# Up products of the experts as three products of split 16-bit halves, in a fused attention and mixture-of-experts kernel

## What is computed

```
logits = xf @ router_w
gate_vals, idx = top_k(logits, 2)
gates = softmax(gate_vals)
for e in range(8):
    h = relu(xf @ w1[e] + b1[e]) @ w2[e] + b2[e]
    y = layernorm(xf + h, gamma[e], beta[e])
    out = out + sum(where(idx == e, gates, 0)) * y
```

## Time and profile before

| | us |
|---|---|
| median of 3 runs | 539.31 |
| the profiled execution, its own time | 539.75 |
| its span, from the first to the last instruction | 538.0 |
| TensorE busy | 482.5 |
| VectorE busy | 440.2 |
| ScalarE busy | 366.8 |
| GpSimd busy | 307.6 |

### The profile page before, as it was taken

One profiled execution on the slowest core, in us unless ns is written; L12 is line 12 of the kernel. 1 busy time (PEld: TensorE's weight loads), 2 busy tenths in 40 slices (PEclk: granted clock), 3 DMA queues, 4 the chain that ended last, 5 costly groups with the idle time before them and its releaser, 6 DMA issues.

```text
span 538.0 us, 15851 instructions
## 1 busy us (share of the span) xinstructions
PE 482.5 (90%) x4764; PEld 389.4 (72%) x4764; DVE 440.2 (82%) x1768; ACT 366.8 (68%) x849; POOL 307.6 (57%) x447
## 2 busy tenths in 40 slices
PE   3989999999999999989999899999999999999700
PEld 2866666767666666666666699999899999999700
DVE  5876877997777697978778669989998888879897
ACT  5566567776756767667577566876686787778562
POOL 2542021557784386576876768777776555545420
PEclk9999999999899999999899999999999999999955
DMA  5247744426154322333311674877897788886499
GB/s 148 76 153 234 232 108 136 125 81 190 34 174 125 115 88 93 108 110 116 124 37 33 175 262 132 220 201 208 245 275 234 210 244 244 248 225 213 151 337 260
DMA packets 73590, 90.43 MB, mean 168 GB/s; under 512 B 9262, under 2 KB 57297, under 8 KB 73506
## 3 DMA queue, kind: packets, MB, share of 16 engines
q1 hardware_dynamic: 52626, 66.43, 43.0%
q0 software_dynamic: 6416, 12.93, 6.8%
q10 hardware_dynamic: 14464, 10.06, 6.2%
HBM read 63.25 MB, written 30.79 MB: 175 GB/s over the span
## 4 chain that ended last, share of the span: by engine, by line
PE 36%; issue 21%; POOL 20%; DVE 14%; ACT 3%; DMA 2%; SPq 1%; ACTq 1%; POOLq 0%; DVEq 0%
PE sbk L985 12%; POOL sorted_d L1685 11%; PE avb L997 6%; PE mbk L997 6%; POOL kept L1662 2%; POOL rs L1671 2%; PE mbk L975 1%; PE mbk L860 1%; PE avb L800 1%; DVE stk L1575 1%; PE sbk L827 1%; DMA xins<-in_xp 1%; PE gen L808 1%; DVE pexs L1457 1%; DVE pexs L1487 1%
## 5 line engine op out<-in xcount | busy, mean ns | idle before, releaser
L1685 POOL DMA_INDIRECT sorted_d<-pay,slot x96 | 96.8, 1008 | 35.8 <-issue 25.1
L1188 DVE TENSOR_REDUCE mx<-mbk 128x4 f32<-128x768 f32 x96 | 91.1, 949 | 30.3 <-PE mbk L860 29.9
L1699 POOL DMA_INDIRECT expert_d<-pexs,dest x70 | 70.3, 1004 | 42.6 <-DVE pexs L1487 24.8
L648 ACT ACTIVATE pexs<-sbk 128x768 f32<-128x768 f32 x96 | 77.5, 808 | 22.7 <-PE sbk L887 21.2
L985 PE MATMUL sbk<-pexs 128*128 128x256 f32 (+1 forms) x224 | 50.6, 369 | 0.3 <-ACT pexs L697 0.3
L985 PE MATMUL sbk<-pexs,stk 128*128 128x256 f32 (+1 forms) x224 | 48.3, 358 | 1.2 <-issue 1.1
L697 ACT ACTIVATE pexs<-sbk,xins 128x256 f32<-128x256 f32 (+1 forms) x112 | 43.9, 463 | 7.8 <-PE sbk L985 5.7
L697 ACT ACTIVATE pexs<-sbk,w12s 128x256 f32<-128x256 f32 (+1 forms) x112 | 42.6, 450 | 8.2 <-PE sbk L985 6.9
L1699 POOL DMA_INDIRECT expert_d<-xT,dest x33 | 32.9, 996 | 21.4 <-issue 10.7
L985 PEld LDWEIGHTS sbk<-pexs 128*128 128x128 f32 x224 | 39.0, 190 | 4.4 <-issue 0.5
L1648 POOL TENSOR_TENSOR kept<-hs,lnb 128x384 f32<-128x384 f32 x16 | 16.0, 1000 | 45.2 <-DVE hs L1163 45.1
(11 more groups left out here) (259 smaller groups left out, 1239.5 us busy)
## 6 DMA issues: line engine op xcount, KB each, us to landing
stk<-pack_d SPq DMA_DIRECT2D x28, 512.0 KB
pexs<-pack_d SPq DMA_DIRECT2D x28, 512.0 KB
stack_d<-kqs ACTq DMA_DIRECT2D x48, 192.0 KB, 2.6
stk<-stack_d SPq DMA_DIRECT2D x64, 144.0 KB
xn<-sorted_d SPq DMA_DIRECT2D x47, 132.0 KB
pack_d<-in_w SPq DMA_DIRECT2D x16, 256.0 KB
xins<-in_xp SPq DMA_DIRECT2D x16, 128.0 KB, 3.9
hs<-in_txt SPq DMA_DIRECT2D x16, 128.0 KB, 3.2
```

The lines of the kernel that those rows point to most:

```text
L648: act.activation(pex[p % 2][m][:, :, :], sbk[:, :, 0:COLS], ACT.Exp, scale=0.25).then_inc(a_pex, 1)
L1188: dve.tensor_reduce(dst, mbk[:, :, 0:COLS].rearrange("p h (c s) -> p h c s", c=2), AX.X, ALU.max).then_inc(d_mx, 1)
L1685: pool.indirect_dma_start(sorted_d[:, :], bass.IndirectOffsetOnAxis(ap=slot[p % 6][:, 2 * k + w:2 * k + w + 1], axis=0), pay[p % 6][:, k, ...
L1699: pool.indirect_dma_start(expert_d[:, :], bass.IndirectOffsetOnAxis(ap=dest[fin % DESTS][:, k:k + 1], axis=0), ye[fin % RESULTS][:, k, :], ...
```

## The change

- `w1` is split. For each expert, SyncE loads `w1[e]` into SBUF (`fetch`), ScalarE scales it by 32 and rounds it to 16 bits (`w1_high`), VectorE computes the rest as another 16-bit half (`w1_low`), and `pack` writes both halves to `pack_d`. The halves together have the size of the 32-bit weights. The eight `w1_high` and `w1_low` are put into the lists of the attention stage, and the next `fetch` stands at the end of `pack`.
- The turned rows are split too: ScalarE writes the high half `xh` (where it wrote `xsT`), and VectorE subtracts it from the turned rows in PSUM and writes the low half `xl` (`low`).
- Each up product becomes three products of 16-bit halves: low weights by high rows, high by high, high by low. Relu divides by 32.
- `first` and `dest` go from VectorE to GpSimd, as three operations (`mark`). ScalarE's `norm_row(g)` now also waits for `mark(g - 4)`, since that reads the expert's number from the same buffer.
- The weights go through 6 buffers in place of 8.

The core of the diff:

```diff
-WEIGHTS, NORMS = 8, 4
+WEIGHTS, NORMS = 6, 4
+RAISE = 32.0
...
+            def fetch(e):
+                if e:
+                    sp.wait_ge(w1_split, 2 * e)
+                sp.dma_start(w1_f32, a["w1"][e]).then_inc(w1_in, 16)
+
             def pack(e):
-                sp.dma_start(pack_d[e, :, 0:F], a["w1"][e]).then_inc(pack_out, 16)
+                sp.wait_ge(w1_split, 2 * e + 2)
+                sp.dma_start(pack_d[e, :, 0:F], plans[:, F:2 * F]).then_inc(pack_out, 16)
                 sp.dma_start(pack_d[e, :, F:F + FC * D].rearrange("p (c d) -> p c d", c=FC),
                              a["w2"][e].rearrange("(c p) d -> p c d", p=P)).then_inc(pack_out, 16)
+                if e + 1 < NE:
+                    fetch(e + 1)
...
+            def w1_high(e):
+                act.wait_ge(w1_in, 16 * (e + 1))
+                if e:
+                    act.wait_ge(pack_out, 32 * e)
+                act.activation(w1_f16[:, 0:F], w1_f32, ACT.Copy, scale=RAISE).then_inc(w1_split, 1)
...
                 after(act, b_y, g - NORMS)
+                after(act, b_dest, g - NORMS, 3)
...
-                    act.activation(xsT[nxt % 2][:, 0:n], (bank[6] if nxt else gen_of("b0", 0))[:, 0:n], ACT.Copy).then_inc(b_xs, 1)
+                    act.activation(xh[nxt % 2][:, 0:n], turned_of(nxt)[:, 0:n], ACT.Copy).then_inc(b_xh, 1)
...
-            xt(3); hi(3); vcopy(2); vcopy(3); lo(3); xt(4); xnorm(5); hi(4); mxt(0); xt(5); gexp(6); lo(4); gexp(7)
+            xt(3); hi(3); vcopy(2); vcopy(3); lo(3); xt(4); xnorm(5); hi(4); w1_high(0); mxt(0); xt(5); gexp(6); lo(4); gexp(7)
...
-            context(1, 1); vcopy(5); soft(2, 1); mxt(3); ct(0); soft(2, 2); soft(2, 3); xnorm(9); context(2, 0)
+            context(1, 1); vcopy(5); soft(2, 1); mxt(3); ct(0); soft(2, 2); soft(2, 3); xnorm(9); w1_high(3); context(2, 0)
...
-                        last = pe.matmul(bank[4 + c // 2][:, (c % 2) * G:(c % 2) * G + n],
-                                         ws[cur % WEIGHTS][:, c * P:(c + 1) * P], xsT[cur % 2][:, 0:n], start=True, stop=True)
+                        up = bank[4 + c // 2][:, (c % 2) * G:(c % 2) * G + n]
+                        high, low = w1[:, c * P:(c + 1) * P], w1[:, F + c * P:F + (c + 1) * P]
+                        pe.matmul(up, low, xh[cur % 2][:, 0:n], start=True, stop=False)
+                        pe.matmul(up, high, xh[cur % 2][:, 0:n], start=False, stop=False)
+                        last = pe.matmul(up, high, xl[cur % 2][:, 0:n], start=False, stop=True)
...
+            def w1_low(e):
+                dve.wait_ge(w1_split, 2 * e + 1)
+                dve.scalar_tensor_tensor(out=w1_f16[:, F:2 * F], in0=w1_f32, scalar=RAISE, in1=w1_f16[:, 0:F], op0=ALU.mult,
+                                         op1=ALU.subtract).then_inc(w1_split, 1)
...
+            def low(g):
+                if g < GRID:
+                    dve.wait_ge(b_xh, g + 1)
+                    after(dve, b_up, g - 2, 2)
+                    n = chunks(g) * P
+                    dve.tensor_tensor(xl[g % 2][:, 0:n], turned_of(g)[:, 0:n], xh[g % 2][:, 0:n], ALU.subtract).then_inc(b_xl, 1)
...
-                    after(dve, b_dest, old - 1)
-                    dve.tensor_scalar(first[:, 0:n], xs[old % 6][:, 0:n, D + 1], nr[old % NORMS][:, AT_ID:AT_ID + 1], None,
-                                      ALU.is_equal).then_inc(b_first, 1)
-                    after_scatters(old - DESTS)
-                    dve.wait_ge(b_first, old + 1)
-                    dve.scalar_tensor_tensor(out=dest[old % DESTS][:, 0:n], in0=first[:, 0:n], scalar=-float(TOKENS),
-                                             in1=xs[old % 6][:, 0:n, D], op0=ALU.mult, op1=ALU.add).then_inc(b_dest, 1)
...
-            reduce_max(0, 5); reduce_max(1, 0); mish1(6); reduce_max(1, 1); mish2(6); mish3(6); reduce_max(1, 2)
+            w1_low(0); reduce_max(0, 5); reduce_max(1, 0); mish1(6); reduce_max(1, 1); mish2(6); mish3(6); reduce_max(1, 2)
...
+            def mark(g):
+                if g < GRID:
+                    n = chunks(g)
+                    after_dma(pool, xs_in, g)
+                    pool.wait_ge(b_nr, g + 1)
+                    after(pool, b_dest, g - 1, 3)
+                    pool.tensor_scalar(first[:, 0:n], xs[g % 6][:, 0:n, D + 1], nr[g % NORMS][:, AT_ID:AT_ID + 1], -float(TOKENS),
+                                       ALU.is_equal, ALU.mult).then_inc(b_dest, 1)
+                    pool.wait_ge(b_dest, 3 * g + 1)
+                    pool.tensor_tensor(target[:, 0:n], first[:, 0:n], xs[g % 6][:, 0:n, D], ALU.add).then_inc(b_dest, 1)
+                    if g >= DESTS:
+                        pool.wait_ge(ye_out[(g - DESTS) % RESULTS], 16 * blocks_to(g - DESTS, chunks(g - DESTS) - 1, RESULTS))
+                    pool.wait_ge(b_dest, 3 * g + 2)
+                    pool.tensor_copy(dest[g % DESTS][:, 0:n], target[:, 0:n]).then_inc(b_dest, 1)
+
             def step_b(old, fin):
+                if 0 <= fin + 1 < GRID:
+                    mark(fin + 1)
...
-                    pool.wait_ge(b_dest, fin + 1)
+                    pool.wait_ge(b_dest, 3 * fin + 3)
```

More of the change, by code:

```diff
@@ L315, in early_fusion @@
         one16 = sb("one16", [P, 2 * NE])
-        past2 = sb("past2", [P, SLOTS - EARLY, 2 * NE])
-        pastn2 = sb("pastn2", [P, SLOTS - EARLY, 2 * NE])
+        plans = sb("plans", [P, 2 * F])
+        assert 2 * (SLOTS - EARLY) * 2 * NE <= 2 * F
+        past2, pastn2 = [plans[:, i * (SLOTS - EARLY) * 2 * NE:(i + 1) * (SLOTS - EARLY) * 2 * NE].rearrange("p (g e) -> p g e", e=2 * NE)
+                         for i in range(2)]
+        w1_f32, w1_f16 = plans[:, 0:F], plans[:, F:2 * F].bitcast(F16)
         second = sb("second", [P, SLOTS - EARLY])
@@ L335, in early_fusion @@
         stk32 = stk[:, :, :, :, :].rearrange("p i s j t -> p (i s j t)").bitcast(F32)
-        ws = [stk32[:, i * (4 * COLS):i * (4 * COLS) + WROW] for i in range(4)] + [flat0[:, i * WROW:(i + 1) * WROW] for i in range(4)]
+        ws = [stk32[:, i * (4 * COLS):i * (4 * COLS) + WROW] for i in range(4)] + [flat0[:, i * WROW:(i + 1) * WROW] for i in range(2)]
         assert len(ws) == WEIGHTS
@@ L347, in early_fusion @@
         hid = [room(1024 * i, (FC, G)) for i in range(2)]
-        xsT = [room(2048 + 256 * i, (G,)) for i in range(2)]
+        xh, xl = [[room(2048 + 256 * i + 128 * j, (G // 2,)).bitcast(F16) for i in range(2)] for j in range(2)]
         z = [room(2560 + 256 * i, (2, D)) for i in range(2)]
@@ L492, in load @@
                 after(sp, b_z, g - 6)
-                after(sp, b_dest, g - 6)
+                after(sp, b_dest, g - 6, 3)
                 n = chunks(g)
@@ L728, in _ @@
             hi(9); context(5, 1); lo(9); vcopy(9); gexp(12); soft(6, 0); mxt(7); xt(10); soft(6, 1); hi(10); lo(10)
-            soft(6, 2); ct(5); payload(4); soft(6, 3); context(6, 0); x2t(4); xnorm(12); soft(6, 4); soft(6, 5)
+            soft(6, 2); ct(5); payload(4); soft(6, 3); context(6, 0); x2t(4); xnorm(12); w1_high(5); soft(6, 4); soft(6, 5)
             soft(7, 0); context(6, 1); vcopy(10); soft(7, 1); mxt(8); soft(7, 2); xt(11); soft(7, 3); payload(5)
@@ L971, in step_b @@
                         after(pe, d_cn, PAIRS - 1)
-                    after(pe, b_xs, nxt - 1)
-                    turned = bank[6] if nxt else gen_of("b0", 0)
+                    after(pe, b_xl, nxt - 1)
                     for k in range(chunks(nxt)):
-                        last = pe.transpose(turned[:, k * P:(k + 1) * P], xs[nxt % 6][:, k, 0:D], ident[:, :])
+                        last = pe.transpose(turned_of(nxt)[:, k * P:(k + 1) * P], xs[nxt % 6][:, k, 0:D], ident[:, :])
                     last.then_inc(b_xt, 1)
@@ L1524, in _ @@
             place(10); stats1(10); top8(0); reduce_max(5, 4); lead(0); top_index(0); stats2(2); choices(0); gates(0)
-            onehot(0); moments2(2); moments1(10); reduce_max(5, 5); ranks(0); weight_y(2); select(0); slots(0); denom(3)
+            onehot(0); moments2(2); moments1(10); reduce_max(5, 5); w1_low(4); ranks(0); weight_y(2); select(0); slots(0); denom(3)
             cnorm(3); stats3(2); top8(1); moments3(2); lead(1); top_index(1); reduce_max(6, 0); choices(1); gates(1)
@@ L1534, in _ @@
             mish4(12); stats3(4); gated1(12); reduce_max(8, 1); moments3(4); gated2(12); reduce_max(8, 2); place(12)
-            stats1(12); moments1(12); reduce_max(8, 3); reduce_max(8, 4); stats2(5); reduce_max(8, 5); moments2(5)
+            stats1(12); moments1(12); reduce_max(8, 3); reduce_max(8, 4); stats2(5); reduce_max(8, 5); w1_low(5); moments2(5)
             reduce_max(9, 0); weight_y(5); reduce_max(9, 1); stats3(5); reduce_max(9, 2); moments3(5); top8(4)
```

48 lines of the change are left out of this document (28 added, 20 removed).

## The result

The changed kernel takes 609.0 us (median of 4 runs, 606.3 to 611.4), the kernel before 540.0 (4 runs on the same chip): the ratio is 1.13, with a 95% interval of 1.120 to 1.133. That is 69 us slower where 19 were forecast, and 41 us above the upper end of the range. The profiled execution took 611.4 us, the longest of the four; its span is 609.7.

What follows compares the result with a forecast made beforehand. GpSimd was taken to set the expert stage's pace, leaving TensorE's gain worthless: 538.0 + 9.8 (marks) + 9 (attention stage) = 556.8 us of span, 558 as median. The range for the whole was 534 to 568.

Steps and rivals of the forecast that it cites:

- `mark` = 0.70 us net: GpSimd, expert stage: three small operations with gaps take 0.80, less 0.10 from a shorter gap ahead of the scatter.
- Marks against GpSimd's free time: Expert stage: marks add 16.4 and 20.3 us, 26.9 us are free, so GpSimd ends tile 51 9.8 us later.
- The Trainium skill's estimate: GpSimd about twice as slow for two inputs: a mark 1.0 us net, giving 15 us more than the forecast.
- The attention stage, 9 us, upper bound 13: Added w1_high and w1_low work and waits: 11 us counted, 9 taken since lists make some good; bounds 4 and 13.
- place 0: Attention stage: VectorE reaches w1_low(0) before ScalarE's w1_high(0) is done, reduce_max(0, 5) 4.5 late; 3 us taken.
- Place 3: Attention stage: ScalarE meets w1_high(3) before fetch(3) has arrived and goes on 6 us late; 5 us taken.
- The other six places: Attention stage: remaining w1_high and w1_low pairs, 0.6 and 0.7 us each on two engines; 0.5 each, 3 us together.
- Rival 1: Expert stage: GpSimd catches up and TensorE's gain stands, needing a mark below about 0.4; 532 us median, chance 0.16.
- rivals 2 to 4: Attention stage absorbs waits, 551 us, chance 0.12; mark about 0.5, 548, chance 0.07; neither price there, 526, chance 0.05.
- My 16 us: Expert stage: gain from TensorE's cheaper up products, 1.3 in place of 1.73 us, if TensorE or VectorE sets the pace.
- Six buffers at nothing: Expert stage: six weight buffers in place of eight cost nothing, since weights queue behind rows that wait longer.
- the end tied to tile 51: End of kernel: results are read back once tile 51's scatters land, so the end moves by the same 9.8 us.

Runs made afterwards that it cites:

- e9_staggered: Changed kernel with w1_high, w1_low and pack moved in the attention lists, and GpSimd's three mark operations done for different tiles in one step: 567.0 us.
- e1: Changed kernel with first and dest made by VectorE again, no mark on GpSimd: 559.1 us.
- e7: Changed kernel with eight rows of norms in place of four, so norm_row(g) waits for the mark of tile g - 8: 606.6 us.
- e4: Changed kernel with first and dest on VectorE again and w1_high, w1_low and pack moved in the attention lists: 545.8 us.
- e8: Changed kernel with destinations on VectorE, moved attention-stage operations, and low cut to 8 columns in place of 256 from tile 2 on: 536.2 us.
- e5: Kernel before with six buffers for the experts' weights in place of eight: 540.5 us.
- e3: Changed kernel with only the places of w1_high, w1_low and pack moved for experts 0, 2, 3, 4 and 7: 594.1 us.
- f1: Changed kernel with destinations on VectorE, moved attention-stage operations, and TensorE adding the rows to the down product in place of VectorE's xb: 546.5 us.
- e10: Kernel before with six weight buffers and a GpSimd copy for each tile ahead of its first scatter, waited for in odd tiles only: 540.2 us.
- e6: Kernel before plus one idle GpSimd operation ahead of each first scatter, a short copy for odd tiles, a long power for even ones: 540.1 us.

## Why the prediction was wrong

The direction was right and the mechanism too; the size was 53 us short in the profiled execution (611.4 for 558.5). By its own terms:

- **`mark` = 0.70 us net: this is the step that failed, worth 40 us.** The operations measured 0.31, 0.20 and 0.19, the gaps between them 0.08 and 0.14: 0.92 for my 0.80. The gap ahead of the scatter makes 0.41: I took the 0.20 that stands behind a power of 0.89 us for what stands behind any operation. It is 0.61 where the last wait ended only one short operation earlier. The trace of before had the row that says so, a send behind a short operation that had waited for GpSimd's own power:

```profile
291.96 0.19 POOL L1673 TENSOR_TENSOR nm<-ve,rs 128x3 f32<-128x3 f32 x1
292.76 1.16 POOL L1685 DMA_INDIRECT sorted_d<-pay,slot  x1 [0.61 <-issue]
```

  I had asked for the nearest row by what it was (an operation ahead of an indirect DMA), and not by what it waited for. My upper bound of 1.0 left this gap out too, and so the range could not hold the time. Two terms I had at nothing: 0.08 ahead of the first operation, and 0.14 a tile for slower scatters.
- **Marks against GpSimd's free time.** The form of this sum holds. Take from the stage's 175.4 us the 26.9 that were free, 148.5; for tiles 1 to 51 at 1.44 us that makes 222, measured 224.9. (Over the 47 full tiles `first` takes 0.37 us in the mean, not the 0.31 of the tile shown; that alone would be 3 us.) With 0.70 the same sum is 184, within 1 us of my +9.8. The break-even is 26.9 / 51 = 0.53 us a tile, and e9_staggered shows the form once more: 194.8 - 148.5 = 46.3, or 0.91 a tile, with hardly an idle time of GpSimd. So this arrangement, with the gaps that a wait adds gone, still doesn't reach it.
- **The Trainium skill's estimate** (GPSIMD Engine Reference, Engine selection), 15 us more than mine, was nearer by luck. The factor of two is stated for operations with two inputs, and I had taken it for all three, of which only one has two. That one took 0.20 and not 0.32, and the surplus lay in a gap that the rule doesn't speak of.
- **The attention stage, 9 us, upper bound 13: 22.6 measured** (18.3 and 23.2 in e1 and e7, with the same lists). This is the second step that failed, worth 14 us. Both places were right, and so were their waits, 5.17 for my 4.3 of VectorE's and 6.38 for my 5.5 ahead of the fetch. Two things were mis-sized. I let half of place 0's wait be absorbed (3 us), while TensorE idled 3 us and then ran 6 us at half its clock, which is another 3: 6.6. Place 3 cost 7.7 between pairs 2 and 3, not 5, with the same 3 us in it (5.6 us of work at half, 114.4 to 120). And "the lists make some good" did not happen: from pair 3 on the shift never fell below 14.9. The other six places and the change of stages make up the rest, 0.6 and 19.2 - 14.9 = 4.3, and then 3.4; my 3 us for the former were a little short, for the latter I had none.
- **TensorE.** The twelve products take 1.3 us as worked out (first at 406.94, the down product at 408.25), and the gain was worth nothing while GpSimd set the pace. Rival 1 needed a mark below 0.4; rivals 2 to 4 fall with the attention stage's 22.6 and the mark's price. e1 and e4 show what the gain is worth without marks, 3.4 us in the late part, and 6.6 if `low` were free as well. My 16 us were too much: VectorE, which I had fitting into 3.3 us a step, is the bound, and even with `low` nearly gone (e8) the whole stage is only 7.3 us shorter than before (168.1 for 175.4), 0.7 of it ahead of tile 28.
- **Six buffers at nothing** and **the end tied to tile 51** were right: 540.5 us in e5; tile 51 ends 72.1 us later and the span is 71.7 longer.

What remains open: what makes TensorE's clock fall at the change of stages. In e4's profiled execution it is at half there, and in e9's too (0.58 and 0.50 in the two stretches of 5 us from 310 on). In e3's and e8's, with the same attention lists, it is at its full level, and in f1's as well, though TensorE is busy only 2.8 of the 5 us from 310 on. So e4's attention lists alone don't decide it, and part of its 9.1 us may belong to that one execution. The two bad places were not tried one at a time. And that some work for the scatter comes after the last wait is inferred from the gaps; no row shows the work itself.

## What to carry to other kernels

Price an operation ahead of an indirect DMA by what the engine last waited for, not by its length: look in the trace for the same chain of waits. If a queue's work on small numbers has to be done by the engine that issues the DMAs, do each step for another tile, so that no wait ends right in front of a DMA. And an engine that the page shows busy 57% can be full: count its gaps first, since free time per tile (here 0.53 us) is what a moved part has to fit into. When a stall of several us is put into TensorE's way, add what the lower clock takes behind it, here 3 us each time.

## What the runs showed of the hardware

- An indirect DMA on GpSimd starts 0.16 us behind a short operation, 0.30 behind another indirect DMA, and 0.77 behind the same short operation if GpSimd has waited for that operation (e10). A wait for another engine does the same: in 22 of the 24 scatters of the kernel before that follow an idle time above 0.7 us, it starts 0.76 to 0.78 us after VectorE's result has ended, as here, 412.98 - 412.21 = 0.77:

```profile
411.60 0.61 DVE L1487 SCALAR_TENSOR_TENSOR xT<-pexs,rs,w12s 128x128 f32<-128x128 f32 x2
```

  So some 0.7 to 0.8 us of work for the DMA seem to come after the last wait, whichever engine it was for, and to be hidden otherwise behind the instruction before. The Trainium skill (DMA: Bandwidth & Descriptors, Latency and other measured facts) gives about 1 us until such a DMA's first byte for the work of making it; the 0.97 to 1.06 us of the DMA_INDIRECT rows are of that size, and the part ahead of them is not in them.
- A copy of two numbers for each partition that nobody waits for costs GpSimd 0.1 us or less between two indirect DMAs in half of the tiles, and 0.22 at most (e6).
- TensorE's clock fell to its lower level during idle times of 3.0 and 6.4 us, and stayed there for another 5.8 and 5.6 us of full work.
